# One patch-embedding and two-block model on one core: in the last stage, the first chunk's projection, norm and first-layer tiles stand ahead of the second chunk's shares, and the third chunk's expert rows stand in the first period

## The reference, cut to what matters

```python
def _L1_attn_ref(x, qkv_w, qkv_b, rpb, proj_w, proj_b):      # K = 7 neighbours, 16 heads
    qkv = (x @ qkv_w.T + qkv_b)...
    attn = einsum('bhld,bhlkd->bhlk', q, k[:, :, idx]) + bias
    attn = softmax(attn)
    return einsum('bhlk,bhlkd->bhld', attn, v[:, :, idx])... @ proj_w.T + proj_b

def _L1_ffn_ref(x, router_w, W1, b1, W2, b2):                # 6 experts of 341, all computed
    expert_weights = ...softmax(x.mean(axis=1) @ router_w.T), two largest, partition table...
    h = gelu(einsum('bsd,edf->ebsf', x, W1) + b1)
    return einsum('be,ebsd->bsd', expert_weights, einsum('ebsf,efd->ebsd', h, W2) + b2)

h = h + _L0_ffn_ref(_layernorm(h), ...)                      # the rows of its experts: y_rows, OG
h = h + _L1_attn_ref(_layernorm(h), ...)
h = h + _L1_ffn_ref(_layernorm(h), ...)
```

## Time and profile before

| | |
|---|---|
| median of 3 runs | 821.22 us (820.77 to 825.59) |
| the profiled execution | 817.75 us |
| its span | 815.9 us |
| mean granted clock of TensorE | 0.874 of full speed |
| busy in the span: TensorE, VectorE | 620.8 us (76%), 621.7 us (76%) |
| busy in the span: ScalarE, GpSimd | 517.0 us (63%), 278.7 us (34%) |

### The profile page before, as it was taken

One profiled execution on the slowest core, in us unless ns is written; L12 is line 12 of the kernel. 1 busy time (PEld: TensorE's weight loads), 2 busy tenths in 40 slices (PEclk: granted clock), 3 DMA queues, 4 the chain that ended last, 5 costly groups with the idle time before them and its releaser, 6 DMA issues.

```text
span 815.9 us, 10867 instructions
## 1 busy us (share of the span) xinstructions
PE 620.8 (76%) x3090; PEld 472.5 (58%) x3091; DVE 621.7 (76%) x1275; ACT 517.0 (63%) x821; POOL 278.7 (34%) x321
## 2 busy tenths in 40 slices
PE   6996751735628173569768899987899999999997
PEld 3564651735628173565546699844556656666565
DVE  1788598999999999999886122267798898896853
ACT  1488899989998999993233134442565565565442
POOL 0464200000000100000387244416357657664642
PEclk9996886958777695869686799999999999999999
DMA  5371042355444455540611366320000000000000
GB/s 183 113 282 63 1 87 51 67 100 106 74 87 87 88 101 102 92 74 6 223 32 37 105 177 187 93 67 1 1 1 9 2 10 10 0 10 10 2 10 18
DMA packets 26384, 56.50 MB, mean 69 GB/s; under 512 B 4204, under 2 KB 15573, under 8 KB 25861
## 3 DMA queue, kind: packets, MB, share of 16 engines
q0 software_dynamic: 5728, 24.56, 16.0%
q1 hardware_dynamic: 19848, 30.80, 12.2%
q10 hardware_dynamic: 764, 0.62, 0.2%
HBM read 29.91 MB, written 10.17 MB: 49 GB/s over the span
## 4 chain that ended last, share of the span: by engine, by line
PE 48%; ACT 18%; DVE 15%; issue 11%; POOL 3%; DMA 2%; POOLq 1%; SPq 1%; ACTq 1%; DVEq 0%
PE psum L2113 6%; PE psum L1895 4%; PE psum L1897 4%; PE psum L1896 4%; PE psum L1809 4%; ACT s_R L899 3%; PE psum L2028 3%; ACT s_R L889 3%; PE psum L2100 3%; PE psum L2036 3%; ACT s_R L894 3%; PE psum L2203 2%; PE psum L2102 2%; PE psum L2101 2%; POOL x_sorted L698 2%
## 5 line engine op out<-in xcount | busy, mean ns | idle before, releaser
L1895 PE MATMUL psum<-s_xn_lo,s_split_hi 128*128 128x368 f32 x256 | 94.9, 371 | 132.5 <-ACT s_R L924 132.5
L1895 PEld LDWEIGHTS psum<-s_xn_lo,s_split_hi 128*128 128x128 f32 x256 | 55.1, 215 | 135.8 <-ACT s_R L924 135.2
L683 POOL DMA_DIRECT2D s_xnfm<-s_R x14 | 17.1, 1219 | 249.9 <-DVE s_R L1310 249.9
L1305 DVE TENSOR_TENSOR_SCAN s_R<-s_R 128x2944 f32<-128x2944 f32 x15 | 94.4, 6292 | 0.7
L1896 PE MATMUL psum<-s_xn_hi,s_split_lo 128*128 128x368 f32 x256 | 92.2, 360 | 0.0
L1897 PE MATMUL psum<-s_xn_hi,s_split_hi 128*128 128x368 f32 x256 | 91.9, 359 | 0.0
L1069 ACT ACTIVATE s_R<-psum,s_cols 128x368 f32<-128x368 f32 x96 | 50.1, 565 | 65.9 <-PE psum L2102 65.8
L2113 PE MATMUL psum<-s_R 128*128 128x368 f32 x256 | 90.5, 484 | 0.0
L742 POOL TENSOR_TENSOR s_R<-s_R 128x368 f32<-128x368 f32 x47 | 54.0, 1148 | 39.5 <-DVE s_R L1601 19.3
L931 ACT ACTIVATE s_R<-psum,s_cols 128x736 f32<-128x736 f32 x64 | 56.0, 875 | 14.2 <-PE psum L1897 10.7
L779 POOL TENSOR_TENSOR s_R<-s_R 128x368 f32<-128x368 f32 x48 | 46.5, 969 | 53.9 <-DVE s_R L1737 53.0
(11 more groups left out here) (263 smaller groups left out, 1608.9 us busy)
## 6 DMA issues: line engine op xcount, KB each, us to landing
s_xnfm<-s_R POOLq DMA_DIRECT2D x14, 1472.0 KB, 10.5
s_R<-in_w SPq DMA_DIRECT2D x28, 256.0 KB
s_R<-in_xg SPq DMA_DIRECT2D x7, 744.0 KB, 4.1
x_sorted<-in_x_init SPq DMA_DIRECT2D x1, 5082.0 KB
s_wBC<-in_wBC SPq DMA_DIRECT2D x8, 256.0 KB, 2.8
s_R<-in_v SPq DMA_DIRECT2D x2, 1024.0 KB
s_R<-x_sorted SPq DMA_DIRECT2D x28, 66.0 KB
s_R<-in_w SPq DMA_DIRECT2D x1, 1536.0 KB, 6.6
```

What stands on the lines that cost most here:

```text
L1305: dve.tensor_tensor_scan(bufB[:, u], ra[:, u], bufB[:, u], 0.0, ALU.mult, ALU.add).then_inc(ra_free, 1)
L1895: pe.matmul(bank(c), w_hi[:, s, u, k, :], xn_lo[:, a:b], start=True, stop=False)
```

## The change

It rewrites the order by hand on four engines; no computation is added or left out, save that eight of the unread matmuls go.

- Period 0: VectorE adds the expert rows of chunk 2, two ahead of `shares_rest` and two behind it, and makes their statistics behind the third offset. GpSimd adds the first chunk's bias ahead of its additions and makes `rstd_e(2)` behind them.
- Period 1: `project(0)` stands behind the q matmul and ahead of k and v, in PSUM bank 5. `residual_stats(0)` stands ahead of the score products. ScalarE norms chunk 2 and chunk 0 and copies the turned chunk 0 (`stream_hi`, bank 4) ahead of the exponential and its table. TensorE turns chunk 0 ahead of `scores_tm`. `split_stream(0)` and `stream_sums(0)` stand ahead of `shares`. First-layer entries 0 to 3 of chunk 0 and the router's logits take the place of `keep_busy(8)`, and entries 14 to 17 move from period 2 to the end of period 1.
- From period 2's projection on, the order is as before.

```diff
@@ -508,6 +508,15 @@
+        def project_bank(f):
+            return 6 if f else 5
+
+        def stream_bank(f):
+            return 5 if f else 4
+
+        def ffn_first(f):
+            return 14 if f else 18
+
         def tile_no1(f, e, j):
@@ -785,10 +794,12 @@
                 add_expert(c - 3, NE)
-                if 1 <= c <= NCH:
+                if 2 <= c <= NCH:
                     projection_bias(c - 1)
-                if c + 1 < NCH:
+                if c != 1 and c + 1 < NCH:
                     rstd_e(c + 1)
+                if c == 0:
+                    projection_bias(0)
                 add_expert(c - 2, 1)
@@ -800,6 +811,8 @@
                     second_share(c - 1)
+                if c == 0:
+                    rstd_e(2)
             stage_end(pool, 5)
@@ -1104,7 +1117,7 @@
                 act.wait_ge(nF.xT_ready, 2 + f + 1)
-                act.activation(fm(xn_hi, f % 2), bank(5), ACT.Copy).then_inc(nF.xT_free, 1)
+                act.activation(fm(xn_hi, f % 2), bank(stream_bank(f)), ACT.Copy).then_inc(nF.xT_free, 1)
@@ -1113,26 +1126,31 @@
                     qkv_out(c)
-                gelus(c - 2, 14, 16)
-                gelus(c - 2, 16, 18)
+                gelus(c - 2, ffn_first(c - 2), 18)
+                if c == 1:
+                    normed_e(2)
+                    normed_f(0)
+                    stream_hi(0)
                 if c < NCH:
...
                 gelus(c - 2, 22, 24)
-                if 1 <= c <= NCH:
+                if 2 <= c <= NCH:
                     normed_f(c - 1)
+                if c == 1:
+                    gelus(0, 0, 2)
                 if c < NCH:
                     shares_out(c)
-                if 1 <= c <= NCH:
+                if 2 <= c <= NCH:
                     stream_hi(c - 1)
...
                     rest_out(c - 2)
-                gelus(c - 1, 0, 6)
+                gelus(c - 1, 2 if c == 1 else 0, 6)
                 if c < NCH:
                     rest_out(c - 2)
-                gelus(c - 1, 6, 12)
+                gelus(c - 1, 6, ffn_first(c - 1) - 2)
                 if c + 1 < NCH:
                     norm_copies(act, nE, c % 2, c + 1, (7, 7))
-                gelus(c - 1, 12, 14)
+                gelus(c - 1, ffn_first(c - 1) - 2, ffn_first(c - 1))
             stage_end(act, 5)
@@ -1539,14 +1557,16 @@
-            def first_experts(c):
+            def first_experts(c, lo=0, hi=CB):
                 dve.wait_ge(og_ready[c % 2], 16 * (c // 2) + 16)
-                for j in range(c * CB, (c + 1) * CB):
+                for j in range(c * CB + lo, c * CB + hi):
                     if j == 2:
...
                                                       ALU.mult, ALU.add))
+
+            def experts_stats(c):
                 step.wait()
@@ -1643,7 +1663,7 @@
                 dve.wait_ge(bias_added, c + 1)
-                step.add(dve.tensor_tensor(seqs(H, c), bank_tm(6), seqs(H, c), ALU.add))
+                step.add(dve.tensor_tensor(seqs(H, c), bank_tm(project_bank(c)), seqs(H, c), ALU.add))
                 step.wait()
@@ -1674,11 +1694,11 @@
                 dve.wait_ge(nF.xT_free, c + 3)
-                dve.tensor_tensor(fm(xn_lo, c % 2), bank(5), fm(xn_hi, c % 2).bitcast(f32), ALU.subtract)\
+                dve.tensor_tensor(fm(xn_lo, c % 2), bank(stream_bank(c)), fm(xn_hi, c % 2).bitcast(f32), ALU.subtract)\
                     .then_inc(xf_split, 1)
...
             def stream_sums(c):
-                dve.tensor_reduce(srep, bank(5).rearrange("p (b l) -> p b l", b=CB), AX, ALU.add)\
+                dve.tensor_reduce(srep, bank(stream_bank(c)).rearrange("p (b l) -> p b l", b=CB), AX, ALU.add)\
                     .then_inc(srep_ready, 1)
@@ -1738,6 +1758,7 @@
             first_experts(0)
+            experts_stats(0)
             for c in range(NCH + 2):
@@ -1747,33 +1768,44 @@
                     weigh_rest(f - 1)
-                if c + 1 < NCH:
+                if c != 1 and c + 1 < NCH:
                     first_experts(c + 1)
+                    experts_stats(c + 1)
+                if c == 1:
+                    residual_stats(0)
                 if att:
...
                 store_chunk(c - 3)
-                if tail:
+                if tail and c != 1:
                     residual_stats(f)
...
                     scores_less_max(c)
+                if c == 1:
+                    split_stream(0)
+                    stream_sums(0)
                 weigh_expert(f - 1, 3)
...
                 weigh_expert(f - 1, 4)
+                if c == 0:
+                    first_experts(2, 0, 2)
                 if att:
...
                 weigh_expert(f - 1, 5)
+                if c == 0:
+                    first_experts(2, 2, CB)
                 for o in range(K):
...
                         offset(c, o)
-                    if o == 0:
-                        if tail:
-                            split_stream(f)
-                            stream_sums(f)
+                    if o == 0 and tail and c != 1:
+                        split_stream(f)
+                        stream_sums(f)
+                    if o == 2 and c == 0:
+                        experts_stats(2)
                     if o == 1 and tail:
@@ -2144,15 +2176,17 @@
                     pe.matmul(bank(b), w_qkv[:, k, :], fm(xfm, c), start=True, stop=True).then_inc(qkv_mm, 1)
+                    if c == 1 and k == 0:
+                        project(0)
             def project(c):
-                if c + 1 < NCH:
+                if 1 <= c < NCH - 1:
                     pe.wait_ge(qkv_ready, (c + 1) * 3 + 1)
-                else:
+                elif c:
                     pe.wait_ge(pb_free, NCH * K)
...
                 for j in range(CB):
-                    ins = pe.matmul(bank_tm(6)[:, j, :], pv[:, c % 2, j * L:(j + 1) * L], w_proj, start=True, stop=True)
+                    ins = pe.matmul(bank_tm(project_bank(c))[:, j, :], pv[:, c % 2, j * L:(j + 1) * L], w_proj, start=True, stop=True)
                 ins.then_inc(proj_mm, 1)
@@ -2219,19 +2253,26 @@
                     qkv_of(c)
-                ffn(f - 1, 14, 16)
-                ffn(f - 1, 16, 18)
-                if tail:
+                ffn(f - 1, ffn_first(f - 1), 18)
+                if tail and f:
                     project(f)
...
                     scores(c)
+                if c == 1:
+                    norm_transposes(pe, nF, 0, 0, (4, 4))
                 ffn(f - 1, 18, 20)
...
                 ffn(f - 1, 20, 22)
-                if c < 2:
+                if c == 0:
                     keep_busy(8)
+                if c == 1:
+                    pe.wait_ge(wF_ready, 8 * 16)
+                    pe.wait_ge(v1_split, 1)
+                    ffn(0, 0, 2)
+                    router_logits(0)
+                    ffn(0, 2, 4)
                 ffn(f - 1, 22, 26)
@@ -2240,11 +2281,9 @@
                 ffn(f - 1, 26, 28)
-                if tail:
+                if tail and f:
                     norm_transposes(pe, nF, f % 2, f, (5, 5))
-                if c == 1:
-                    pe.wait_ge(wF_ready, 8 * 16)
-                    pe.wait_ge(v1_split, 1)
+                ahead = ffn_first(f) - 14
                 for o in range(K):
@@ -2256,28 +2295,30 @@
                     elif 1 <= o <= 3:
-                        if o == 1:
+                        if o == 1 and c == 1:
+                            ffn(f, 4, 6)
+                        elif o == 1:
                             ffn(f - 1, 28, 30)
...
                         else:
-                            ffn(f, 2 * o - 2, 2 * o)
+                            ffn(f, 2 * o - 2 + ahead, 2 * o + ahead)
                     elif o == 4:
...
                     elif o == 5:
-                        ffn(f, 6, 8)
+                        ffn(f, 6 + ahead, 8 + ahead)
                     elif o == 6:
...
                             router_spread(f)
-                        ffn(f, 8, 12)
+                        ffn(f, 8 + ahead, 12 + ahead)
                     if o == 1 and tail and not att:
...
                     norm_transposes(pe, nE, c % 2, c + 1, (7, 7))
-                ffn(f, 12, 14)
+                ffn(f, 12 + ahead, 14 + ahead)
                 if tail and not att:
...
             result_last()
```

## The result

| | before | after |
|---|---|---|
| median, us (20 runs each) | 821.00 | 824.27 |
| lowest to highest | 819.38 to 825.59 | 820.76 to 827.22 |
| profiled execution: time, span | 817.75, 815.9 | 821.91, 820.0 |

The ratio is 1.0031, 95% interval 1.0017 to 1.0046: 2.5 us slower by the ratio, 3.3 by the medians, inside the forecast's range and within 1%. The interval lies wholly above 1, so it is slower, by a third of a per cent.

The account below looks back on a forecast made before the run. TensorE nearly full from period 2 on, period 1 loose with a chain of waits across engines; +1.5 at period 2 less 0.4 gives about +1.1 on the 821.22 median: 822.3, eight in ten 818.5 to 825.8.

Parts of the forecast that it names:

- scores' transposes: TensorE, period 1: start at 571.8 instead of 569.51, behind the first chunk's norm; softmax of chunk 1 2.3 us late.
- shares' transposes: TensorE, period 1: 2.9 us late, of which 2.3 are the norm, 0.4 the split and 0.2 the gelus.
- The blocked rstd: Period 1: GpSimd's first rstd instruction of chunk 0 held until VectorE's nine products end, some 3.2 us; chance 0.45.
- Rival 1: Period 1: GpSimd gets in between two products, so the softmax starts where it did; -0.9 us, 820.3; chance 0.2.
- The statistics in period 0: VectorE, between third and fourth offset: chunk 2's statistics make GpSimd's later additions 0.6 us late, bounds 0 and 1.3.
- The half of 0.9 us: Period 2: products take 0.9 us less if GpSimd is the one blocked; half counted, 0.4 off, bounds 0 and 0.9.
- +1.5 at the q of period 2: Start of period 2: 2.9 us late less 1.1 to 1.6 regained, so 1.3 to 1.8 late, near 591.7.
- The expert additions' 3.07 us: VectorE: chunk 2's four additions leave period 1 and cost nothing in period 0, hidden in two waits; bounds 0 and 3.07.
- replaced by a chain 0.7 us longer: Start of period 1: 4.4 us off VectorE replaced by a GpSimd, TensorE, VectorE chain; products start 0.7 us late.
- 1.00 from 530 on: TensorE's granted clock, expected full from 530 on in the changed profile; less under rival 2.
- rival 2: Period 1: TensorE's clock falls as filler is gone; 2.5 to 3 us on top, 825; chance 0.22.
- Rival 3: Both removals land in full, 4.4 us of VectorE less 0.7 and 2.7 us of tiles: 815 to 817; chance 0.1.

Follow-up runs that it names:

- fill2: Changed kernel with filler matmuls where TensorE waits, as fill, but none ahead of the first chunk's projection and one more behind the shares' transposes; 821.54 us, ratio 0.9987.
- experts_stay: fill2 with chunk 2's expert rows, statistics and rstd back in period 1, ahead of the first chunk's residual; 821.07 us, ratio 0.9967.
- let_in2: let_in without the four fillers behind the scores; 820.85 us, ratio 0.9985.
- norm_behind: experts_bias plus the change's projection and residual places; first chunk's norm, split and tiles stay in the order of before; 819.00 us, ratio 0.9957.
- experts_bias: experts_fill with the first chunk's projection bias moved to period 0 and two more fillers where TensorE waited for the split; 817.95 us, ratio 0.9944.
- experts_alone: Kernel before with only chunk 2's expert additions, statistics and rstd moved from period 1 to period 0; 821.39 us, ratio 0.9999.
- tiles_back: Changed kernel with the first chunk's first-layer tiles 14 to 17 back in period 2; 824.40 us, ratio 1.0037.
- fill: Changed kernel with filler matmuls put back where TensorE waits, including one ahead of the first chunk's projection; 820.81 us, ratio 0.9979.
- let_in: fill2 with one wait more: VectorE waits for the first chunk's rstd before the products of period 1; 822.99 us, ratio 1.0010.
- experts_fill: experts_alone with the filler of before_fill; 820.00 us, ratio 0.9979.
- before_fill: Control: kernel before with filler matmuls added where TensorE waits, its own eight staying; 820.83 us, ratio 0.9982.

## Why the prediction was right

The time came inside the range. The steps of the order came near where the forecast had them, the clock did not stay where it had it, and the last digit is luck. The table of profiles with a clock of 1.00 in both periods:

| | period 0 | period 1 | to before |
|---|---|---|---|
| before | 21.15 | 30.51 | |
| fill2: changed order | 21.50 | 31.24 | +1.08 |
| experts_stay | 21.17 | 31.78 | +1.29 |
| let_in2 | 21.47 | 30.97 | +0.78 |
| norm_behind | 21.47 | 30.22 | +0.03 |
| experts_bias | 21.48 | 28.78 | -1.40 |

Read from the bottom, the table gives the order in three parts: expert rows and bias -1.40, the projection and the residual ahead of the products +1.43, the norm and the tiles ahead of the softmax +1.05, in sum +1.08. Each part is the difference of two profiles.

**The order.** Forecast +1.1 in all; fill2 has +1.08. Step by step, behind the q of period 1 (forecast, fill2): residual 2.47, 2.56; products 4.37, 4.48; scores' transposes 11.6, 11.62; shares' transposes 17.6, 17.54; q of period 2 31.5, 31.24. The blocked rstd, the case I gave 0.45, came in all six profiles of this order in which VectorE went straight from the first chunk's statistics to the products (3.21 to 3.24 us). Rival 1 did not.

**What was off within it.** The statistics in period 0 were put at 0.6 us and cost 0.35. The half of 0.9 us that I took off in period 2 did not come: GpSimd was first there again (596.14, 0.19 us, in the changed kernel) and the products took 3.99. The stretching isn't that of the rstd, either, as I had read it. In the kernel before six of the seven took 0.51 us, and one 1.43, from 594.23 to 595.66, while GpSimd's addition for the second network's experts (742) ran:

```profile
592.52 3.99 DVE L1640 TENSOR_TENSOR s_R<-s_R 128x344 f32<-128x344 f32 x7
...
594.32 0.96 POOL L742 TENSOR_TENSOR s_R<-s_R 128x368 f32<-128x368 f32 x1
```

In period 4 of that profile the rstd was in first as well and this addition came behind the products, and they took 3.07. So the forecast had 0.25 too much in period 0 and 0.26 too much in period 1 (31.5 against 31.24), and its +1.5 at the q of period 2, with bounds 1.3 and 1.8, is +1.08 in fill2: outside them. It then took 0.4 off that never came. That the two cancel to 0.02 us is luck. The expert additions' 3.07 us, counted as gone, were right on VectorE, and at nothing in their new place too: in the changed kernel the first offset starts 14.81 us after the q of period 0, as before. But the step "replaced by a chain 0.7 us longer" hides how little the removal was worth behind that chain: 0.2 us (experts_stay).

**The clock.** The forecast rested on 1.00 from 530 on, a fall priced at nothing, and this step failed in the profiled execution: rival 2 happened besides, 2.26 us where I had put 2.5 to 3. Its place was half right. The second fall came 0.1 us after the end of the 2.56 us wait for the copies. But the first was earlier, round the q of period 1, ahead of all that is ordered anew there. It came in all three profiles that have the statistics of chunk 2 between two offsets and no filler ahead of the transposes of nE (changed kernel, experts_alone, tiles_back), in none of the four with the order of before in period 0, and in one of seven with the statistics and filler (fill). This says which orders the first fall came with; how it comes about stays open. I had looked for idle TensorE only where the change names it. The median of 824.27 is above the 821.6 to 823.1 of the forecast's own case and nearer to rival 2's 825 than to 822.3. How it divides between order and clock in a typical execution is not shown: the medians' clocks (0.867 against 0.868 to 0.869) are nearly the same, as the kernel before has falls too. An estimate from the ratios: filler took the changed kernel from 1.0031 to 0.9979 and 0.9987, 3.6 to 4.3 us, and the kernel before to 0.9982, 1.5 us. The difference, 2 to 3 us, would be what the changed order loses to the clock beyond the kernel before, and the intervals are nearly as wide.

**Rival 3** would have needed both removals to land. Tiles: TensorE's busy share of 29.22 in 30.80 spoke for it, and period 2 took 30.82, 30.83 before; they were worth nothing there. Expert rows: they land, with the bias 1.73 us in period 1, only if the first chunk's projection and residual don't stand in front (experts_bias, 28.78); with these in front alone period 1 is 30.22 (norm_behind).

The Trainium skill (SBUF — State Buffer, "Who interferes with whom") has the two engines exclude each other for one instruction. The six blocked first instructions each span the nine products, 3.07 plus 0.36 us in fill2, so going by the row was right for them. Other rows do go by the page. The product of 1.43 us waited out one addition of 0.96. And in experts_bias the fourth rstd instruction took 0.35 us for its 0.20 and ended 0.06 us behind one product, with four still to come:

```profile
564.44 0.35 POOL L753 TENSOR_TENSOR s_R<-s_R,s_rs 92x4 f32<-92x4 f32 x1
```

Why the first one is held for the whole run, and the fourth isn't, stays open. let_in, where the products waited and the instruction took 0.19 us, agrees with the page that it is the products that hold it off.

## What to carry to other kernels

A removal from a busy engine is worth what the next chain in line leaves of it: moved alone with the bias, the expert rows gave 1.4 us, behind the projection's chain 0.2. Whoever moves work ahead of a softmax moves every wait of that work ahead of it too, on each in-order queue (1.05 us here). And where filler matmuls stand, count them as part of the kernel: look where each move opens a gap on TensorE, also in the period before, and compare orders in profiles at the same clock before trusting a difference of 3 us.

## What the hardware showed

- In a low stretch in which TensorE is full the loss is real: experts_fill and experts_bias have period 1 of 33.36 and 28.78 us, with 10.2 us of low clock in the first and none in the second (they differ by the bias and one filler too). Where waits lie in it, 13.7 us of it came with 2.26 (changed kernel against fill2).
- A wait of TensorE of 1.11 to 1.14 us in front of the offsets had a fall within 1.2 us of its end in fill, before_fill, experts_fill and experts_alone, one after 2.4 us in tiles_back, and none in before (1.11) and in the changed kernel (1.14). With filler in its place (experts_bias, norm_behind) there was none. But in let_in the clock fell at 590.0 without such a wait. So a fall isn't certain after a wait, nor excluded without one, and single profiles differ by 3 to 5 us through it (33.35 and 35.50 against 30.51).
- GpSimd's first rstd instruction, 92x4 elements, waited out the whole run of VectorE's nine products (3.21 to 3.24 us) where it started 0.16 to 0.20 us after the first of them. Where it started 0.08 us after (before, 654.30) it took 0.21, and 0.19 where it was in first or VectorE was waiting. An instruction that came later in the run, 0.35 us in experts_bias, waited for one product only.
- One product waited out a longer GpSimd instruction: 1.43 us beside an addition of 0.96 (before, 594.23), 1.59 beside the bias of 1.54 (experts_fill), where the others took 0.51. That is the 3.99 and the 4.15 us of the seven against 3.07; beside the rstd alone they took 3.07 (experts_bias).
